# One-core transformer stack on Trainium2: once-folded sequences with eight transform blocks, the reciprocal root on two columns, later places of the chunk stages

## The reference, cut to what matters

```python
x = x + _layernorm(_L0_attn_ref(_layernorm(x), Wq, Wkv, Wo, bo))          # causal attention, 32 heads of 16
x = x + _layernorm(_L0_ffn_ref(_layernorm(x), gate_t, up_t, down_t, ...)) # hidden 1792, integer weights with scales
x = x + _layernorm(_L1_attn_ref(_layernorm(x)))
x = x + _layernorm(_L1_ffn_ref(_layernorm(x), gate_w, up_w, down_w, ...)) # hidden 1376, low-rank additions

def _L1_attn_ref(x):                      # row by row, L = 512
    f = jnp.fft.rfft(xh, axis=-1)
    corr = jnp.fft.irfft(f * jnp.conj(f), n=L, axis=-1)
    weights, delay = jax.lax.top_k(corr, 6)
    tmp_corr = jax.nn.softmax(weights, axis=-1)
    # sum over the six delays of tmp_corr * x rolled by the delay
```

## Time and profile before

| what | value |
|---|---|
| median of 3 runs | 921.38 us (920.71 to 922.01) |
| the profiled execution's own time | 920.06 us |
| its span | 918.0 us |
| TensorE busy | 749.4 us (82%) |
| VectorE busy | 670.1 us (73%) |
| ScalarE busy | 363.9 us (40%) |
| GpSimd busy | 291.7 us (32%) |
| all transforms and correlations (L1183) | 40.4 us in 336 matmuls |
| the root's two lines (L245, L249) | 66.3 us in 336 instructions |

### The profile page before, as it was taken

How to read it: one execution, slowest core, us unless ns; L and a number is a source line. 1 busy time by engine, 2 the same in 40 slices (tenths; PEclk the granted TensorE clock), 3 DMA queues, 4 the chain that set the end, 5 groups by cost and what they waited for, 6 DMA issues and landing times. The chain is left out here.

```text
span 918.0 us, 16061 instructions
## 1 busy us (share of the span) xinstructions
PE 749.4 (82%) x5081; PEld 408.7 (45%) x5102; DVE 670.1 (73%) x1781; ACT 363.9 (40%) x699; POOL 291.7 (32%) x348
## 2 busy tenths in 40 slices
PE   1967666879898898988869998696969999788694
PEld 1623221223222222222327676474747777566472
DVE  7523875766776767797489999896998999955713
ACT  1212224545565545677104444343433534323121
POOL 4024443102021120232104555345524335224131
PEclk9988656989899999998979999898989999899798
DMA  9499889772131312644451375613645221110100
GB/s 265 74 177 341 237 245 225 150 165 60 29 60 28 49 39 39 154 121 135 107 159 25 98 141 109 187 24 86 81 98 94 43 35 25 24 46 1 46 24 24
DMA packets 144477, 93.38 MB, mean 102 GB/s; under 512 B 111832, under 2 KB 123224, under 8 KB 144200
## 3 DMA queue, kind: packets, MB, share of 16 engines
q1 hardware_dynamic: 133360, 70.19, 34.4%
q10 hardware_dynamic: 10816, 16.91, 5.9%
q0 software_dynamic: 240, 5.51, 2.9%
HBM read 48.47 MB, written 29.04 MB: 84 GB/s over the span
## 5 line engine op out<-in xcount | busy, mean ns | idle before, releaser
L1205 PE MATMUL ps<-arena 128*128 128x256 f16 (+1 forms) x1952 | 238.2, 279 | 23.9 <-DMA arena<-arena 23.9
L1205 PEld LDWEIGHTS ps<-arena 128*128 128x128 f16 (+1 forms) x1952 | 196.4, 101 | 68.5 <-DMA arena<-arena 16.9
L1432 ACT ACTIVATE arena<-ps 128x1024 f32<-128x1024 f32 (+7 forms) x256 | 163.6, 651 | 123.4 <-PE ps L1462 118.8
L1453 PE MATMUL ps<-arena 96*128 (+4 forms) x384 | 137.0, 382 | 39.9 <-DVE mx L1369 15.5
L1365 DVE CUSTOM_DVE_ANT_0 arena<-ps,arena 128x256 bf16<-128x256 f32 (+3 forms) x256 | 122.0, 488 | 57.2 <-PE ps L1453 49.4
L1057 POOL TENSOR_TENSOR arena<-arena 128x256 f32<-128x256 f32 (+1 forms) x100 | 80.3, 803 | 258.3 <-ACT arena L948 257.6
L1227 PE MATMUL ps<-arena 128*128 128x512 f16 (+2 forms) x467 | 119.6, 385 | 32.6 <-POOL arena L1063 31.2
L1462 PE MATMUL ps<-arena 99*128 (+4 forms) x384 | 128.6, 352 | 4.6 <-ACT arena L1432 4.2
L1340 POOL TENSOR_SCALAR_AFFINE_SELECT arena<-arena 128x512 f32<-128x512 f32 x64 | 42.2, 659 | 230.4 <-ACT arena L1432 230.2
L1369 DVE TENSOR_REDUCE mx<-ps 128x1 f32<-128x512 f32 x128 | 88.2, 689 | 32.1 <-PE ps L1453 31.2
L1453 PEld LDWEIGHTS ps<-arena 96*128 (+1 forms) x384 | 39.3, 102 | 150.0 <-issue 81.0
(11 more groups left out here) (163 smaller groups left out, 851.9 us busy)
## 6 DMA issues: line engine op xcount, KB each, us to landing
arena<-qp_d SPq DMA_DIRECT2D x48, 128.0 KB, 4.1
lora_d<-arena ACTq DMA_DIRECT2D x20, 256.0 KB, 4.5
arena<-lora_d SPq DMA_DIRECT2D x10, 512.0 KB, 5.1
w1n_d<-arena SPq DMA_DIRECT2D x10, 512.0 KB, 3.6
arena<-rec_d SPq DMA_DIRECT2D x32, 128.0 KB, 2.6
qp_d<-arena SPq DMA_DIRECT2D x12, 256.0 KB, 4.9
w1dn_d<-arena SPq DMA_DIRECT2D x4, 704.0 KB, 3.8
arena<-in_L_ffn_down_w_dram ACTq DMA_DIRECT2D x16, 172.0 KB, 3.6
```

Of the source, the lines that this page charges most:

```text
L1205: last = nc.tensor.matmul(ps[0:h, b, CH * o:CH * (o + 1)], w(t[0])[:, kt, ht * P:ht * P + h], xt[:, c, t[1], kt, :], start=(kt, t) == (0, ...
L1432: nc.scalar.activation(probs[:, kt % 2, h, kt * P:T], st_bank(h).rearrange("p b n -> p (b n)")[:, kt * P:T], ACT.Exp, scale=HD ** -0.5).th ...
L1453: nc.tensor.matmul(s_bank(g, u)[:, 0:k1 - k0], qt6[0:QROWS, g % RING, h, qt * P:(qt + 1) * P], kt6[0:QROWS, g, k0:k1], start=True, stop=Tr ...
```

## The change

The sequences are folded once: `fold` and `unfold` lose the second fold, `FORWARD` has eight blocks, `BACK` two halves of 256 columns from two blocks each, and the tables follow. `moments` calls `rsqrt` on both columns in place of `rsqrt_by_column`. The stages of chunks 0 to 3 move to later tiles, by none to three tiles, in the lists of TensorE, ScalarE and GpSimd alike (`LAGS_AT` by three each). `odd` goes; folded rows are made from `expc` into `y`, and the lag weights are written in place in `expc`, so `lag_terms` waits for the pieces of the chunk before (`nat_ready`). The inverse table lies in two places and is loaded in two parts, later.

```diff
-FORWARD = ((0, 0), (0, 1), (1, 2), (2, 0), (2, 1), (3, 3))
-BACK = (((0, 0), (2, D // 2), 0, D // 2), ((1, D), D // 2, P), ((3, D + P), D // 2 + P, P))
+FORWARD = ((0, 0), (0, 1), (1, 2), (1, 3), (2, 0), (2, 1), (3, 2), (3, 3))
+BACK = (((0, 0), (2, D // 2), 0), ((1, D), (3, D + D // 2), D // 2))
...
-        ROWS_AT = (26, 45, 64, 76)
-        CORR_AT = (28, 49, 65, 77)
-        LAGS_AT = (30, 53, 66, 78)
-        SPEC_AT = (39, 59, 71, 82)
-        PROD_AT = (43, 61, 73, 84)
-        BACK_AT = (47, 62, 74, 86)
+        ROWS_AT = (26, 46, 66, 77)
+        CORR_AT = (28, 49, 68, 78)
+        LAGS_AT = (33, 56, 69, 81)
+        SPEC_AT = (40, 61, 73, 85)
+        PROD_AT = (45, 63, 75, 87)
+        BACK_AT = (48, 65, 76, 88)
...
+            sp.dma_start(inv_sb[0], inverse[0]).then_inc(tables_loaded, 16)
             down_load(sp, 0)
+            sp.dma_start(inv_sb[1], inverse[1]).then_inc(inverse_loaded, 16)
...
-            link(nc.vector.tensor_scalar(var[:, 0:SUB], mv[:, 0:SUB, 1], LN_EPS, -0.5, ALU.add, ALU.mult))
-            rsqrt_by_column(link, SUB)
+            link(nc.vector.tensor_scalar(var[:, 0:SUB], mv[:, 0:SUB, 1], LN_EPS, None, ALU.add))
+            rsqrt(link, SUB)
...
-        def fold(link):
+        def fold(link, of):
 
-            low, high = y[:, :, 0:H2], y[:, :, H2:D]
-            link.later(nc.vector.tensor_tensor(odd, low, high, ALU.subtract))
-            link(nc.vector.tensor_tensor(low, low, high, ALU.add))
-            rising, falling = odd[:, :, 1:P], odd[:, :, H2 - 1:P:-1]
-            link.later(nc.vector.tensor_tensor(y[:, :, H2 + 1:H2 + P], rising, falling, ALU.subtract))
-            link.later(nc.vector.tensor_tensor(y[:, :, H2 + P:D - 1], rising, falling, ALU.add))
-            link(nc.vector.tensor_copy(y[:, :, H2:D:H2 - 1], odd[:, :, 0:H2:P]))
+            low, top_half = of[:, :, 0:H2], of[:, :, H2:D]
+            link.later(nc.vector.tensor_tensor(y[:, :, 0:H2], low, top_half, ALU.add))
+            link(nc.vector.tensor_tensor(y[:, :, H2:D], low, top_half, ALU.subtract))
 
         def unfold(dve, link, c):
 
-            z = wback
             dve.wait_ge(back_taken, SUB * (c + 1))
-            even, cosine, sine = z[:, :, 0:H2], z[:, :, H2 + 1:H2 + P], z[:, :, H2 + P:D - 1]
-            link.later(nc.vector.tensor_tensor(odd[:, :, 1:P], cosine, sine, ALU.add))
-            link.later(nc.vector.tensor_tensor(odd[:, :, H2 - 1:P:-1], sine, cosine, ALU.subtract))
-            link(nc.vector.tensor_copy(odd[:, :, 0:H2:P], z[:, :, H2:D:H2 - 1]))
+            even, odd = wback[:, :, 0:H2], wback[:, :, H2:D]
...
                 if c:
-                    act.wait_ge(pick_done, k - 1)
+                    act.wait_ge(nat_ready, SUB * (use_of("lags", c - 1) + 1))
```

More of the change, by code:

```diff
@@ L235, in rsqrt @@
                                                     op0=ALU.add, op1=ALU.mult))
[L238 to L251, removed]
         XS, WS, TS = 2.0 ** 10, 2.0 ** 8, 2.0 ** 10
@@ L609, in ffn_pieces @@
         def ffn_pieces(dve, link, c):
-            normalised_rows(link, c)
-            fold(link)
+            normalised_rows(link, c, expc)
+            fold(link, expc)
             pieces(dve, link, use_of("ffn", c))
@@ L798, in lag_weights @@
                 dve.wait_ge(e_ready, k + 1)
-                nc.vector.scalar_tensor_tensor(out=y[:, i, :], in0=picked[:, 0:D], scalar=PICKED, in1=expc[:, i, :],
+                nc.vector.scalar_tensor_tensor(out=expc[:, i, :], in0=picked[:, 0:D], scalar=PICKED, in1=expc[:, i, :],
                                                op0=ALU.is_equal, op1=ALU.mult).then_inc(pick_done, 1)
                 dve.wait_ge(pick_done, k + 1)
-            fold(link)
+            fold(link, expc)
             pieces(dve, link, use_of("lags", c))
@@ L1174, in back @@
             for i in range(SUB):
-                for *parts, to, width in BACK:
-                    product(pe, ps[:, 2 + i, to:to + width], lambda w, k: sqp[:, c % 2, w, k[0], i * P:(i + 1) * P],
-                            lambda r, k: inv_sb[:, r, k[1]:k[1] + width], b_ready if to + width == D else None, parts)
+                for *parts, to in BACK:
+                    product(pe, ps[:, 2 + i, to:to + D // 2], lambda w, k: sqp[:, c % 2, w, k[0], i * P:(i + 1) * P],
+                            lambda r, k: inv_sb[r][:, k[1]:k[1] + D // 2], b_ready if to else None, parts)
         def product(pe, to, lhs, rhs, ready, parts=range(ND)):
@@ L1774, in tables @@
     even, odd = 2 * np.arange(P), 2 * np.arange(P) + 1
-    low, rising, falling = n[:half], n[:P], n[1:P + 1]
+    low = n[:half]
     cosines, sines = np.cos(angle(low, even)), np.sin(angle(low, even))
     sines[:, 0] = np.cos(angle(low, [half]))[:, 0]
-    forward = np.concatenate([cosines, np.cos(angle(rising, odd)), sines, np.sin(angle(falling, odd))], 0)
+    forward = np.concatenate([cosines, np.cos(angle(low, odd)), sines, np.sin(angle(low, odd))], 0)
     twice = np.where(even == 0, 1.0, 2.0)[:, None] / D
@@ L1783, in tables @@
     back = np.concatenate([twice * np.cos(angle(even, low)), -2.0 / D * np.sin(angle(even, low)),
-                           2.0 / D * np.cos(angle(odd, rising)), -2.0 / D * np.sin(angle(odd, falling))], 1)
+                           2.0 / D * np.cos(angle(odd, low)), -2.0 / D * np.sin(angle(odd, low))], 1)
     power[half] = nyquist
```

21 lines of the change are left out of this document (10 added, 11 removed).

## The result

The changed kernel takes 937.65 us, the median of 4 runs (935.37 to 940.87); the kernel before took 921.69 us beside it (4 runs, 920.71 to 923.33). The ratio is 1.019 with a 95% interval of 1.015 to 1.022: slower by about 16 us. The forecast was 928.6 us, slower by 7.2, with a range that ends at 938.0. The sign was right and the size was not.

What follows compares the result with a forecast made beforehand. VectorE's and TensorE's in-order lists were taken to bound the kernel by turns, around `rolled`. Tile 56 coming 15.7 us earlier and +22.9 us behind it gave +7.2 on the 921.38 us median: 928.6 us, range 914.5 to 938.

Steps and rivals of the forecast that it cites:

- Tile 56: Start of tile 56, which waits for `rolled(0)`: 666.0 us, 15.7 earlier, set by VectorE; TensorE ready at 657.7.
- the loss of 5 us by the root: VectorE ahead of tile 56: ten reciprocal-root calls beside GpSimd, each 0.5 us slower, +5.0 us.
- the prediction's sign of being wrong: Tile 56 before 660 us, or root instructions at 0.17 us throughout, or TensorE without a gap at tile 67.
- The root: VectorE's two-column reciprocal root: +0.5 us a call in the first layer's stretch, 0 in the second, -0.78 where GpSimd idles.
- rival 2: VectorE's root excluded by GpSimd for whole instructions, +1.3 us a call in the first layer: 937 us at most, chance 0.12.
- Tile 56 to tile 67: TensorE, 63.4 us (before 51.5): 8.8 for two tiles, 27.4 for seven, products 5.2, then 22 behind `back(1)`.
- Tile 67 to tile 78: TensorE, 68.7 us (before 58.05): 45.7 for tiles, restart, correlation, products and ScalarE's peaks, then 23 behind `back(2)`.
- Tile 78 to tile 89, and the end: TensorE, 67.7 us (before 66.5) including 21.5 behind `back(3)`; then 59.4 to the end (before 60.2).
- The larger products and the folds: TensorE's transforms and `back`: 7.8 us more; VectorE's folds and `unfold` up to `rolled(0)`: 6.8 us less.
- The first: VectorE's root seldom blocked by GpSimd, gaining 0.78 us at every call; tile 56 at about 657: 914.6 us, chance 0.13.
- The third: Later places cost nothing, as TensorE finds its rows ready at tiles 67 and 78: 911.9 us, chance 0.07.
- The fourth: Whole kernel: gains and losses cancel within noise, with lower root prices and tails 1.5 us shorter: 921 us, chance 0.08.

Runs made afterwards that it cites:

- fold alone: The changed kernel with the places of before and the root by columns, so only single fold and eight blocks against the kernel before: 916.04 us, ratio 0.995.
- root undone: The changed kernel with `rsqrt_by_column` back in `moments`: 948.31 us, ratio 1.031 to the kernel before.
- root alone: The kernel before with the reciprocal root on both columns and nothing else changed: 913.50 us, ratio 0.994.
- old places: The changed kernel with the six tuples of places of the kernel before; folds, blocks and root as changed: 911.84 us, ratio 0.992.
- late places alone: The kernel before with the later places only; two folds, six blocks and root by columns stay: 947.64 us, ratio 1.031.
- the exponentials earlier: The changed kernel with `correlate(2)` at tile 67 instead of 68 and the exponentials of its peaks at 67 instead of 69: 924.90 us, ratio 1.007.
- first half's places: The kernel before with only the later places of chunks 0 and 1 that act ahead of tile 56: 919.91 us, ratio 0.998.

## Why the prediction was right in sign and half in size

**Tile 56 (666.0 forecast, 663.42 measured).** The mechanism held: no gap above 2.24 us at the peaks of chunks 0 and 1, and tile 56 stands directly behind a transposing DMA. VectorE's last piece of `rolled(0)`, the row that answers to the first of the earlier trace rows:

```profile
657.24 1.29 DVE L651 TENSOR_TENSOR arena<-arena 128x512 f16<-128x512 f32 x2
```

It ends at 658.5 us instead of 666.9, 8.4 us earlier where the forecast had 4.9; the loss of 5 us by the root did not occur (below), and as the surplus is only 3.5, other terms of the sum must have brought less than forecast; no run shows which. The transposes land 4.9 us behind it and not 4.0. The two errors leave 2.6. TensorE arrives at 660.8 (663.42 - 2.58), where the forecast had 657.7, so TensorE's own lead is 2.6 us and not 8.3, and the tile is still set by VectorE and the transposes. The hit within 2.6 us is in part luck: in the six kernels that are alike up to here tile 56 starts at 657.5, 659.4, 663.4, 663.9, 664.4 and 669.3 us, so a single execution could also have shown 660 or less, the prediction's sign of being wrong.

**The root (+0.5 us a call beside GpSimd, 0 in the second layer; measured about nothing and a gain).** This step failed too: it had a price where there is none, and nothing where there is a gain. By lines, 484 to 670 us, first the changed kernel, then the kernel before (busy, mean ns, idle before):

```profile
L231 DVE SCALAR_TENSOR_TENSOR nw<-nw,var 128x2 f32<-128x2 f32 x33 | 8.9, 269 | 1.1
L233 DVE SCALAR_TENSOR_TENSOR rstd<-nw,rstd 128x2 f32<-128x2 f32 x33 | 8.8, 268 | 1.1
L230 DVE TENSOR_TENSOR nw<-rstd 128x2 f32<-128x2 f32 x33 | 7.2, 218 | 1.1
```

```profile
L245 DVE TENSOR_SCALAR nw<-rstd,var 128x1 f32<-128x1 f32 x66 | 15.0, 269 | 1.2
L249 DVE TENSOR_SCALAR rstd<-nw,rstd 128x1 f32<-128x1 f32 x66 | 11.0, 209 | 1.2
```

and the same three lines of the changed kernel between 670 and 860 us:

```profile
L231 DVE SCALAR_TENSOR_TENSOR nw<-nw,var 128x2 f32<-128x2 f32 x29 | 5.2, 180 | 1.0
L233 DVE SCALAR_TENSOR_TENSOR rstd<-nw,rstd 128x2 f32<-128x2 f32 x28 | 4.9, 176 | 1.0
L230 DVE TENSOR_TENSOR nw<-rstd 128x2 f32<-128x2 f32 x29 | 4.7, 161 | 1.0
```

Nine instructions of 0.252 us on average and 0.033 between them are 2.57 us in the first stretch, what nine of them had been priced at 2.86 to 3.3. Taken over the whole call in VectorE's timeline, from the seed instruction to whatever follows the root, a call takes 2.98 us before (11 calls) and 2.85 after (11 calls) in the first stretch, 2.86 (12 calls) and 2.23 (10 calls) in the second. So -0.1 and -0.6 us a call where the forecast had +0.5 and 0. Two more executions of each form say about the same: by columns 2.98 and 3.01 in the first stretch, 2.93 and 2.93 in the second (fold alone, root undone); on both columns 2.93 and 2.97, then 2.48 and 2.80 (root alone, old places). What failed is the choice of the nearest row. The neighbours of the earlier trace rows, at 307 and 360 ns, are means of 11 instructions each, made of short ones (the medians are 169 and 170 ns) and of 10 in 22 that are over 230 ns. Of the chained ones in the changed kernel's first stretch only 19 of 99 are over 230 ns, and the median is 161. The same two neighbours in the changed kernel between 670 and 860 us, where the root itself is nearly undisturbed:

```profile
L525 DVE TENSOR_SCALAR var<-mv 128x2 f32<-128x2 f32 x10 | 3.8, 380 | 0.3
L227 DVE TENSOR_SCALAR rstd<-var 128x2 int32<-128x2 int32 x10 | 3.4, 338 | 0.3
```

They are longer there than the nine behind them by a factor of two (8 of 20 over 230 ns, against 2 of 86), so they were no measure of the root's own length.

The instructions on two columns are not immune (218 to 269 ns beside 161 to 180 in a stretch where GpSimd is less busy), so there is something of an exclusion. In the eight profiled kernels with the root on both columns, 484 to 860 us, 211 of 1608 chained instructions are over 230 ns, and every one of them ends within 0.06 us of the end of a GpSimd instruction, as in the earlier trace rows. By the Trainium skill, page "SBUF — State Buffer", section "Who interferes with whom", VectorE instructions with two SBUF inputs and GpSimd's that read SBUF exclude one another for whole instructions. The traces are in line with that rule met now and then, and speak against it met whole, which was rival 2.

**Tile 56 to tile 67 (63.4 forecast, 63.9 measured).** The gap ahead of tile 67 was to be about 10 us and is 12.09; VectorE was to idle about 5 us ahead of `rolled(1)` and about 10 ahead of the peaks of chunk 2. Its timeline:

```profile
705.60 0.69 DVE L638 TENSOR_TENSOR arena<-arena 128x512 f32<-128x512 f32 x1 [4.42 <-ACT arena L987]
...
734.84 0.43 DVE L760 TENSOR_SCALAR arena<-ps 128x257 f32<-128x257 f32 x1 [11.46 <-PE ps L1160]
...
742.41 0.69 DVE L775 SCALAR_TENSOR_TENSOR arena<-arena 128x512 f32<-128x512 f32 x1 [3.13 <-ACT arena L962]
...
749.26 0.69 DVE L582 TENSOR_TENSOR arena<-ps,row_b 128x512 f32<-128x512 f32 x1
...
750.60 0.67 DVE L582 TENSOR_TENSOR arena<-ps,row_b 128x512 f32<-128x512 f32 x1
...
769.88 0.42 DVE L793 TENSOR_TENSOR arena<-arena 128x256 f32<-128x256 f32 x1 [8.77 <-ACT arena L972]
```

4.42 and 11.46 us: both right, and the reason too: the chain of chunk 1 moved earlier (`back(1)` by two tiles) brought the gap down from 9.39 to 2.11 us. That the whole step comes out within 0.5 us is in part luck. The forecast counted no gain from the root behind tile 56 but 0.8 us at the end; with the root by columns, which is that premise, the steps 56 to 67, 78 to 89 and 89 to the end take 65.2, 69.6 and 60.5 us, each 1.1 to 1.9 above its forecast. The gain of the root that was left out made up for that.

**Tile 67 to tile 78 (68.7 forecast, 79.5 measured).** This is the step that failed and holds the whole miss. The sum was nine tiles, one restart, the correlation, the products, 0.7 for ScalarE at the peaks and the tail of 23. It says that `correlate(2)` now has to wait for tile 67, and follows that wait along `rolled(2)` only. But VectorE's list has another entry behind `peaks(2)` and `lag_weights(2)`: `ffn_added(3)`, which reads the first layer's last down products out of their bank. `pe_down` of tile 67 writes the next ones into the banks of that walk and waits for `y_free`. The timeline above shows VectorE idle for 11.46 us at the peaks and 3.13 at the exponentials (ScalarE has those in front of tile 69), and only at 751.27 done with L582. Before, VectorE and TensorE met like this:

```profile
740.52 0.69 DVE L598 TENSOR_TENSOR arena<-ps,row_b 128x512 f32<-128x512 f32 x1
...
741.86 0.67 DVE L598 TENSOR_TENSOR arena<-ps,row_b 128x512 f32<-128x512 f32 x1
```

```profile
744.74 1.46 PE L1227 MATMUL ps<-arena 128*128 128x512 f16 x6
```

VectorE was done at 742.53 and TensorE came at 744.74: 2.2 us of margin, with no bracket behind the row, so a reading of the waits alone cannot show it. The gap of 8.82 us costs 8.82 and the slow restart behind it, (2.72 - 1.46) + (3.48 - 2.78) = 1.96, together 10.8 us. Forecast and measurement differ by 10.8. It lies where the wait is: `back(2)` ends 56.8 us behind the start of tile 67 (784.1) where the sum had 45.7, and from there to tile 78 it takes 22.7 us where the sum had 23. The experiments that move the correlation and the exponentials show it: with both 13.3 us go from this segment (8.82, 1.96 and the 2.7 of correlation that hide), with the correlation alone 3.2. No run moved `ffn_added(3)` itself ahead of the peaks, which would test the bank without anything else.

**Tile 78 to tile 89, and the end (67.7 and 59.4 forecast, 66.9 and 59.9 measured).** The gap ahead of tile 89 was to be 17 us and is 15.81. The products of the two spectra in chunk 3 wait 9.66 us instead of 7.84:

```profile
840.24 0.42 DVE L793 TENSOR_TENSOR arena<-arena 128x256 f32<-128x256 f32 x1 [9.66 <-ACT arena L972]
```

**The larger products and the folds.** They were costed at 7.8 us of TensorE and 6.8 us of VectorE up to `rolled(0)`. Together they bring about -5 us (the fold alone); how that splits between the two engines was not tried.

**The rivals.** The first (the root gains everywhere) was right about the sign of the root, but its 914.6 us hung on the second half behaving as forecast; the root's gain was there and the time was 23 us above. The second (lock met whole) comes nearest in time, 937, by luck: its mechanism did not occur. The third (the later places cost nothing) falls with the late places alone, +28 us. The fourth (gains and losses cancel, 921) falls with the result.

**Still open.** Why the chained instructions of the root are stretched less often than their neighbours where GpSimd works less (2 of 86 against 8 of 20) was not measured by itself. Nor was why tile 0 starts anywhere between 472 and 485 us, which is more than most effects looked at here; the medians of 10 runs average over it, a single profile does not.

## What to carry to other kernels

When a stage is moved to a later place in one engine's list, go through everything that stands behind it in the lists of the engines that serve it, not only along the chain that the stage belongs to: a small read that frees a bank stood behind two entries that were made to wait, and it cost 10.8 us. A margin in an in-order list (2.2 us here) shows in no wait of the trace; it has to be made by comparing the end of the freeing instruction with the start of the one that needs it. And where a gap is taken out of one engine, the next engine's list must have room for it: here the later places paid only together with a shorter VectorE list, and then only where the tile that waits for the chunk did not stand close behind.

## What the runs showed of the hardware that was not expected

Instructions with two SBUF inputs on 128x2 numbers, chained one behind the other, take 161 ns each (the median) in every profiled kernel that has them. Some are stretched, to 1.3 us at most, and those end within 0.06 us of an instruction of GpSimd: 158 of 791 between 484 and 670 us, where GpSimd is busy for 99.7 of 186 us in the changed kernel, and 53 of 817 between 670 and 860 us, where it is busy for 62.1 of 190. Their means are 230 to 272 ns in the first stretch and 166 to 221 in the second; those by columns keep 269 and 209 ns in both. So a root of nine chained instructions on both columns is about as fast beside a busy GpSimd as twelve by columns (2.85 to 2.97 against 2.98 to 3.01 us a call), and faster elsewhere (2.23 to 2.80 against 2.86 to 2.93).

A gap of TensorE costs more than its length. The 24 matmuls behind it take 4.80 us after 12.09 idle, 4.33 after 2.58, 4.46 after 3.88, 5.30 after 7.60, but 2.79 after 2.11 and after 1.92, against 2.78 with no gap. In all the kernels of the table, behind 660 us, they take 4.08 to 5.30 us after idles of 2.58 to 17.44 us, and the price does not grow with the gap: 5.30 after 3.58, 4.14 after 7.67. Around 2 us the length alone does not decide: the 24 narrower matmuls of `back(1)` in the first half's places take 3.81 us after 2.17 idle, against 2.14 undisturbed. The clock shows the same from its side. At the new gap of the changed kernel TensorE is idle from 742.6 to 751.42 us; the granted clock is 1.00 of full speed up to 744 us (2.4 GHz), 0.50 from 746 to 754 (1.2 GHz), over the rest of the gap and the first matmuls behind it, and 1.00 again from 756. Where the gap is gone (the exponentials earlier) it is 1.00 from 740 to 754 us.
